# A three-sublayer RWKV-style kernel on 8 cores: the two projections of the feed-forward half in the other order, and one product of the layer norm on another engine

## What is computed

```python
def _layernorm(x, axis=-1, eps=1e-5):
    m = jnp.mean(x, axis=axis, keepdims=True)
    v = jnp.var(x, axis=axis, keepdims=True)
    return (x - m) / jnp.sqrt(v + eps)

# feed-forward (ffn)
xr = mu_r * x + (1.0 - mu_r) * x_prev
xk = mu_k * x + (1.0 - mu_k) * x_prev
r = jax.nn.sigmoid(jnp.einsum('btc,dc->btd', xr, W_r))
k = jnp.einsum('btc,dc->btd', xk, W_k)
k_act = jnp.square(jax.nn.relu(k))
out = r * jnp.einsum('btc,dc->btd', k_act, W_v)

# attention: k, v, r from three mixes and three projections, then a
# recurrence over the tokens (wkv) with a decay per head
return r * wkv @ Wo.T

# the whole
x = x + 0.5 * ffn(_layernorm(x))      # F1
x = x + attn(_layernorm(x))           # A
x = x + 0.5 * ffn(_layernorm(x))      # F2
```

## Time and profile before

| | us |
|---|---|
| timed runs | 3693.35 and 3828.75 (median 3761.05) |
| the profiled execution | 3692.26 |
| its span on the slowest core (core 4) | 3690.7 |
| spans of the eight cores | 3683.0 to 3690.7 |
| busy PE, DVE, ACT in the span | 1779.2, 1548.2, 792.8 |
| mean granted TensorE clock of the cores | 0.716 to 0.718 of full speed |

### The profile page before, as it was taken

The page is one execution under the profiler, slowest core; times in us unless marked ns, Lnnn a source line. Parts: engine busy times, 40 slices in busy tenths (PEclk is TensorE's granted clock), DMA queues, the critical chain, the costliest instruction groups (busy, mean ns, idle before and its releaser), DMA issues.

```text
span 3690.7 us, 24971 instructions; the slowest of 8 cores (3683.0 to 3690.7 us)
## 1 busy us (share of the span) xinstructions
PE 1779.2 (48%) x7063; PEld 779.0 (21%) x7192; DVE 1548.2 (42%) x3658; ACT 792.8 (21%) x1318; POOL 6.5 (0%) x11
## 2 busy tenths in 40 slices
PE   2454545444554545445444545454454545454544
PEld 1222222221221212222122222122222222221222
DVE  1444444434443344443444443444444444434443
ACT  1222222222212222122221222222222222222211
POOL 0000000000000000000000000000000000000000
PEclk9667767776776777767776777777677767777777
DMA  9000000000000000000000000000000000000000
GB/s 165 14 12 12 0 12 12 12 12 8 4 12 12 12 12 0 12 12 12 12 6 6 12 12 12 12 0 12 12 12 12 1 12 12 12 12 12 1 6 12
DMA packets 18213, 49.98 MB, mean 14 GB/s; under 512 B 2593, under 2 KB 2722, under 8 KB 18082
## 3 DMA queue, kind: packets, MB, share of 16 engines
q0 software_dynamic: 7280, 14.68, 2.6%
q1 hardware_dynamic: 6194, 16.92, 1.4%
q10 hardware_dynamic: 4608, 16.78, 1.1%
HBM read 46.27 MB, written 16.78 MB: 17 GB/s over the span
## 4 chain that ended last, share of the span: by engine, by line
PE 47%; DVE 23%; ACT 14%; issue 10%; DVEq 3%; DMA 1%; ACTq 1%; POOL 0%; POOLq 0%
PE p L359 20%; PE p L357 19%; PE p L300 4%; DVE xr L333 3%; PE p L484 3%; PE p L481 2%; DVE s1F L252 2%; ACT junk L246 2%; DVE dbuf L328 2%; DVE xk L333 2%; ACT zfF L311 2%; ACT ka_fm L408 2%; DVE z_tmF L277 1%; DMA fwvt_s<-fwvt 1%; DVE Aprime L505 1%
## 5 line engine op out<-in xcount | busy, mean ns | idle before, releaser
L359 PE MATMUL p<-fwvt_s,ka_fm 128*128 128x512 bf16 x512 | 271.7, 531 | 262.9 <-ACT ka_fm L408 214.5
L300 PE MATMUL p<-idb_s,z_tmF 128*128 128x128 bf16 x512 | 64.7, 306 | 612.0 <-DVE z_tmF L277 612.0
L359 PE MATMUL p<-fwrt_s,xr 128*128 128x512 bf16 x512 | 261.8, 511 | 174.9 <-DVE xr L333 147.4
L357 PE MATMUL p<-fwrt_s,xr 128*128 128x512 bf16 x479 | 248.3, 518 | 151.8 <-DVE xr L333 151.8
L357 PE MATMUL p<-fwvt_s,ka_fm 128*128 128x512 bf16 x449 | 240.2, 535 | 55.3 <-ACT ka_fm L408 55.3
L357 PE MATMUL p<-fwkt_s,xk 128*128 128x512 bf16 x512 | 193.8, 379 | 92.0 <-ACT esig L378 92.0
L414 DVE TENSOR_TENSOR u_sb<-recbF,p 128x512 f32<-128x512 f32 x64 | 44.0, 688 | 428.2 <-PE p L359 423.7
L357 PE MATMUL p<-wkt_s,xk 128*128 128x512 bf16 x225 | 119.0, 529 | 160.1 <-DVE xk L333 159.9
L359 PE MATMUL p<-fwkt_s,xk 128*128 128x512 bf16 x511 | 193.5, 379 | 0.0
L246 ACT ACTIVATE junk<-R 128x1024 bf16<-128x1024 f32 x96 | 100.9, 1051 | 394.5 <-DVE R L417 355.8
L300 PEld LDWEIGHTS p<-idb_s,z_tmF 128*128 128x128 bf16 x512 | 49.5, 137 | 641.5 <-issue 641.5
(11 more groups left out here) (114 smaller groups left out, 3173.7 us busy)
## 6 DMA issues: line engine op xcount, KB each, us to landing
R<-x SPq DMA_DIRECT2D x32, 512.0 KB, 3.2
out<-R ACTq DMA_DIRECT2D x32, 512.0 KB, 2.6
fwrt_s<-fwrt POOLq DMA_DIRECT2D x1, 2048.0 KB, 18.9
fwkt_s<-fwkt POOLq DMA_DIRECT2D x1, 2048.0 KB, 36.4
fwvt_s<-fwvt POOLq DMA_DIRECT2D x1, 2048.0 KB, 48.9
wkt_s<-wkt POOLq DMA_DIRECT2D x1, 2048.0 KB, 61.4
wvt_s<-wvt POOLq DMA_DIRECT2D x1, 2048.0 KB, 72.9
wrt_s<-wrt POOLq DMA_DIRECT2D x1, 2048.0 KB, 85.4
```

The source lines that it names most:

```text
L300: last = t.transpose(p0bank[:, cc * 128:(cc + 1) * 128], src[:, cc * 128:(cc + 1) * 128], idb[:])
L357: t.matmul(pa[:], lhsbuf[:, cc * 128:(cc + 1) * 128], wv[:, cc, 0:512], start=st, stop=sp)
L359: last = t.matmul(pb[:], lhsbuf[:, cc * 128:(cc + 1) * 128], wv[:, cc, 512:1024], start=st, stop=sp)
```

## The change

Two edits. In layer_norm the product negmib moves from ACT to DVE, ahead of z_tm; the drain that stood between Exp and the product on ACT goes, and one comes between the product and z_tm on DVE. meanb now holds the mean with its own sign, and the product carries a -1.0. A branch for a sum that is handed in (s1_ev) comes in; every caller passes None.

In ffn_a the projection with fwkt, with its relu and square, now comes before the projection with fwrt and its sigmoid; the two mixes swap as well.

```diff
         def v12(v):
-            v.reduce_sum(L["s1"][:], R[:], axis=AX.X)
-            v.drain()
-            v.tensor_scalar(L["meanb"][:], L["s1"][:], -1.0 / C, None,
-                            ALU.mult)
+            if s1_ev is None:
+                v.reduce_sum(L["s1"][:], R[:], axis=AX.X)
+                v.drain()
+                v.tensor_scalar(L["meanb"][:], L["s1"][:], 1.0 / C, None,
+                                ALU.mult)
+            else:
...
         def s2f(s_):
             s_.activation(L["lnvb"][:], L["varb"][:], AF.Ln)
             s_.drain()
-            s_.activation(L["invb"][:], L["lnvb"][:], AF.Exp, scale=-0.5)
-            s_.drain()
-            return s_.mul(L["negmib"][:], L["invb"][:], L["meanb"][:])
+            return s_.activation(L["invb"][:], L["lnvb"][:], AF.Exp,
+                                 scale=-0.5)
...
         def v3(v):
+            v.tensor_scalar(L["negmib"][:], L["invb"][:], L["meanb"][:], -1.0,
+                            ALU.mult, ALU.mult)
+            v.drain()
             return v.tensor_scalar(z_tm[slot][:], R[:], L["invb"][:],
                                    L["negmib"][:], ALU.mult, ALU.add)
...
     def ffn_a(i, R, slayer, r_ev, s1_ev=None):
...
-        evmr, evmk = mixes(slayer, i, [(xr_b, "murt"), (xk_b, "mukt")], evev)
+        evmk, evmr = mixes(slayer, i, [(xk_b, "mukt"), (xr_b, "murt")], evev)
+        evk = proj(xk_b, "fwkt", p5, p6, evmk)
+        def srelu(s_):
+            s_.activation(krelu[:, 0:512], p5[:], AF.Relu)
+            return s_.activation(krelu[:, 512:1024], p6[:], AF.Relu)
+        emit("s", srelu, grp="act", waits=[evk], inc="s")
+        e = ev("s")
+        mark_rd(p5, e); mark_rd(p6, e)
+        def vka(v):
+            return v.tensor_mul(ka_tm[:], krelu[:], krelu[:])
+        emit("v", vka, waits=[e], inc="v")
+        evka = ev("v")
         evr = proj(xr_b, "fwrt", p5, p6, evmr)
         def sesig(s_):
...
         evrec = ev("s")
-        evk = proj(xk_b, "fwkt", p5, p6, evmk)
...
-        emit("v", vka, waits=[e], inc="v")
-        return ev("v"), evrec
+        return evka, evrec
```

More of the change, by code:

```diff
@@ L251, in v12 @@
         def v12(v):
-            v.reduce_sum(L["s1"][:], R[:], axis=AX.X)
-            v.drain()
-            v.tensor_scalar(L["meanb"][:], L["s1"][:], -1.0 / C, None,
-                            ALU.mult)
+            if s1_ev is None:
[4 more added lines that the diff above has]
+            else:
+                v.tensor_scalar(L["s1"][:], L["s1"][:], L["s1b"][:], None,
+                                ALU.add)
+                v.drain()
+                v.tensor_scalar(L["meanb"][:], L["s1"][:], 1.0 / C, None,
+                                ALU.mult)
             v.tensor_scalar(L["varb"][:], L["s2"][:], 1.0 / C, None, ALU.mult)
```

## The result

The changed kernel takes 3744.05 us (median of 7 runs) against 3692.87 us: ratio 1.0139, 95% interval 1.0124 to 1.0154. That is 51 us more, a small but certain loss, inside the predicted range (3672 to 3775), but not what was forecast: the forecast was no change, at 3700.

What follows compares the result with a forecast made beforehand. Bound: a chain of handovers between PE, DVE and ACT, no engine full. Plain sum +37.0 - 7.7 = +29.3 us (3721.6), taken as swallowed by the clock except two to three misses, +8 us: 3700 us, no change; range 3672 to 3775.

Steps and rivals of the forecast that it cites:

- What bounds the kernel: Whole kernel: no engine is full; a chain of handovers through PE (47%), DVE (23%) and ACT (14%) sets the time.
- The norm, 0.08 us less each: Layer norm, Exp to z_tm: 0.66 us instead of 0.74, 96 norms, 7.7 us less; new product priced like the m2b step.
- The end of ffn_a in F2, 1.12 us more in 33 places: ka_fm copy waits behind esig, denb and recbF on ACT: 5.64 us to fwvt against 4.52, 37.0 us in all.
- F1 at no cost beyond it: F1's ffn_a: both ends meet the scan, where DVE's t2b waits 3.77 us for PE, so the reordering costs 0 there.
- The plain sum, +29 us: Whole kernel: +37.0 - 7.7 = +29.3 us if nothing is swallowed; as a rival 3721.6 us, chance 0.15.
- The tile of some 112.6 us in spite of the delay: Steady token tile: stays at 112.6 us, whether the edit costs 1.12 or gains 0.08 us.
- The halving from block to block: Cold projection blocks: a start d later ends d/2 later, so 1.12 us is gone after one tile.
- the count of misses: F1's fwvt, starting 0.24 us later each tile, misses its clock rise two to three more times through small hitches: +8 us.
- The price: A block that misses its clock rise stays cold for longer and costs its tile 3.16 us.
- The proof by one tile: F2 transposes at 1135.67 waited 2.73 instead of 2.34 us, yet that tile supposedly took 112.60: the 0.39 us were gone.
- The rival of slower steps: F1's fwvt misses its rise in every tile: 27 more tiles at 3.16 us, 3777 to about 3785 us; chance 0.13.
- the rule that the rise follows a monitor running free of the kernel: Cold blocks: the clock's rise would not move with a late block, leaving a time near that of before.

Runs made afterwards that it cites:

- Experiments 2 and 4: In that order, act_delay (3748.57 us) and copy_early (3613.16 us).
- after_f1_filled: The changed kernel with 16 spare matmuls on PE in F1, between the transposes of ka_tm and fwvt: 3684.48 us, ratio 0.9967 to the kernel before.
- norm_only: The kernel before with the norm edit alone (negmib on DVE, new sign of meanb), projections in their old order: 3681.16 us, ratio 0.9957.
- before_warm: The kernel before with spare matmuls filling PE's long waits from tile 1 on: 3370.77 us, ratio 0.9122.
- order_only: The changed kernel with the norm as before, so only the order of the projections changes: 3751.4 us, ratio 1.0167.
- act_delay: The kernel before with one extra ACT instruction of 128x1024 ahead of the ka_fm copy in F2: 3748.57 us, ratio 1.0139.
- copy_early: The changed kernel, but in F2 ACT copies ka_fm ahead of Ln and Exp of the sigmoid: 3613.16 us, ratio 0.9775 to the kernel before.
- delay_half: The kernel before with one extra ACT instruction of 128x512 (about 0.5 us) ahead of the ka_fm copy in F2: ratio 1.0088 (1.0047 to 1.0129).
- the warm kernels: The kernel before (3370.77 us), the changed kernel (3409.9 us) and copy_early (3298.16 us), each with spare matmuls filling PE's long waits from tile 1 on.

## Why the prediction was wrong

What bounds the kernel: right. The chain of handovers, not an engine, sets the time; shares of the chain are unchanged.

The norm, 0.08 us less each: right, 0.07 measured. m2b was the right row for the new product (0.21 busy, 0.29 to the next).

The end of ffn_a in F2, 1.12 us more in 33 places: right: from esig to fwvt the prediction's terms add up to 5.63 us, and 5.63 was measured, with ACT's order as the cause. F1 at no cost beyond it: right, DVE's t2b still waits for PE, 3.89 us here against 3.77 in the earlier trace rows:

```profile
3488.06 1.44 DVE L502 TENSOR_TENSOR t2b<-p,wtab 128x260 f32<-128x260 f32 x4 [3.89 <-PE p L494]
```

Experiments 2 and 4 show from both sides that the copy's place behind Ln and Exp is what the order of the projections costs.

The plain sum, +29 us, is what these add to, and it is not what was measured. The tile of some 112.6 us in spite of the delay held in the short tiles and, in after_f1_filled, in all of them. The halving from block to block by which the prediction got there was not measured block by block.

**The step that failed is the count of misses: "I take two to three more misses, +8 us".** The price stood: 3.16 us from the earlier trace rows, and the two groups of the changed kernel are 115.9 - 112.9 = 3.0 us apart. The number was wrong by a factor of five: thirteen more long tiles in 28. At 3.0 us each they make 39 of the 51 us; the 28 tiles of a core add up to 3208.3 us in the mean of the cores against 3164.1, 44 more, and the rest lies in the first two tiles, the last one and what follows it. The prediction had estimated that the delay left at F1's fwvt is 0.24 us, had seen that 0.38 us sufficed for a miss, and then treated the 0.14 us between them as a margin that only hitches would use up. But the kernel before stood near the edge already: its own small hitches (0.15 to 0.4 us, about one in each tile) cost it 3 misses in 28 tiles, and norm_only shows how near it was, since an advance of 0.07 us at each norm made all three go. Nor does the wait ahead of the block decide alone: in the changed kernel a block with the same wait as its neighbour (7.85 us) missed. By what rule a given block catches its rise or misses it no run shows.

The proof by one tile ("the 0.39 us were gone") looked at the wrong tile. The late transposes of 1135.67 lie behind this r16ln and ahead of the one at 1182.57:

```profile
1067.22 0.23 ACT L515 ACTIVATE r16ln<-numb 128x16 f32<-128x16 f32 x1 [11.83 <-DVE Aprime L505]
```

So their own tile took 115.35 us, and the tile of 112.60 us is the one that follows; it could have that length whether the 0.39 us had been swallowed or had arrived whole. That a delay is swallowed came out right all the same, but it is after_f1_filled that shows it, and the prediction had no row for it.

The rival of slower steps had the right mechanism and block, and was priced as all or nothing: every tile long, 3785 us, from some 0.3 to 0.4 us on. What came lies between: long and short tiles in turn, 127 long of 224. That case was not on the list.

Of the Trainium skill, page "TensorE: Matmul & The Clock Gate", section "What's actually happening", the rule that the rise follows a monitor running free of the kernel agrees with after_f1_filled (tiles of 112.2 to 113.0 with the lasting delay in them) and with the separate tile lengths of before and after; the tile of 112.60 us that the prediction gave for it has no bearing. The same page's table of the two states (idle is cold, busy is warm) agrees with before_warm, granted clock 0.96, but not with the scan shown in the last section, where the granted clock fell from 1.00 to 0.50 with PE busy.

## What to carry to other kernels

Where blocks start cold behind waits and rise inside, look at the lengths of the loop's rounds before adding up handovers. If they take only two or three values, an edit is worth the change in how many rounds take each value. That depends on how near the weakest block is to missing its rise: a few long rounds already in the trace are a warning that it is near, and counting the cold matmuls of each block in short and long rounds tells which block it is. When two pieces of work change places, follow each engine's queue to the piece that the next matmul waits for: the loss here was one copy that stood behind two activations which nothing needed yet, and the repair brought more than the loss. And a matrix engine that waits half its time may be worth filling with spare matmuls: here that alone took 9% off.

## What the runs showed of the hardware that I had not expected

- Tile lengths go by a ladder: 109.2 to 109.7, 112.1 to 113.6 and 115.2 to 116.6 us in six kernels without spare matmuls (before, after, norm_only, order_only, act_delay, copy_early), and of 6 x 224 tiles none between (each 224 being 28 tiles seen on eight cores). delay_half is not among the six: cores 4 to 7, with the lower granted clock, also show 114.3 us and 117 to 120.
- 0.07 us earlier at three places of a tile took 12 to 16 us off the kernel (norm_only), and 0.96 us later at one place put 53 on (act_delay); 1.97 us earlier at that place took 80 off (copy_early, with the norm's edit).
- Spare matmuls on all eight cores held the granted clock at 0.96 and PE busy for 82% of the span without making the matmuls that count slower: they still show 0.38 us.
- The clock fell during the float32 scan although PE was busy all through it. Two stretches of one scan in the changed kernel (columns as above), with PE busy for the whole of both and the clock at 1.00 and then 0.50:

```profile
3482.20:3485.80 3.60, 3.60 (x13) 1.57 (x12) 0.70 (x1) 2.56 (x4) 0.00 (x0) 1.00 0.00 0
3486.00:3487.80 1.80, 1.80 (x4) 0.55 (x3) 0.00 (x0) 0.44 (x1) 0.00 (x0) 0.50 0.00 0
```

That the scan keeps F1's fwvt fragile, in the warm kernels too, is likely from this but was not tried.
